# The drive of each scan made on VectorE instead of GpSimd, in a two-layer Mamba, MoE and attention kernel

## The reference

```python
def step(state, xs):
    d_t, B_t, C_t, u_t = xs
    dA = jnp.exp(d_t[..., None] * A)
    state = state * dA + (d_t * u_t)[..., None] * B_t[:, None, :]
    y_t = jnp.einsum('ben,bn->be', state, C_t)
    return (state, y_t)
```

## Time and profile before

| | before |
|---|---|
| median of 3 runs | 905.98 us |
| the profiled execution | 904.61 us |
| its span in the profile | 902.4 us |
| PE busy | 736.9 us (82%) |
| DVE busy | 719.1 us (80%) |
| ACT busy | 436.1 us (48%) |
| POOL busy | 388.9 us (43%) |
| DVE scans, L1002 | 32, 99.1 us, mean 3.10 us |
| DVE read-outs, L1020 | 32, 65.5 us, mean 2.05 us |
| POOL drives, L1365 | 32, 97.8 us, mean 3.06 us |

### The profile page before, as it was taken

How to read it: one execution, slowest core, us unless ns; L and a number is a source line. 1 busy time by engine, 2 the same in 40 slices (tenths; PEclk the granted TensorE clock), 3 DMA queues, 4 the chain that set the end, 5 groups by cost and what they waited for, 6 DMA issues and landing times.

```text
span 902.4 us, 10282 instructions
## 1 busy us (share of the span) xinstructions
PE 736.9 (82%) x3448; PEld 563.3 (62%) x3448; DVE 719.1 (80%) x1151; ACT 436.1 (48%) x836; POOL 388.9 (43%) x291
## 2 busy tenths in 40 slices
PE   5256643577666889999978999998999989899997
PEld 1011112345434667888767888887788877688886
DVE  6999988799999977878758877778777757766665
ACT  5444102544542335444455667675666655433442
POOL 0555545365645233445434545455435524221231
PEclk8667675887978999999999999999979999999999
DMA  6132230334335324444410111111110223433340
GB/s 190 57 101 97 72 105 29 97 122 140 121 112 157 113 89 127 152 146 147 133 49 24 57 32 48 42 46 32 30 43 30 74 56 128 130 106 111 100 131 25
DMA packets 40531, 81.33 MB, mean 90 GB/s; under 512 B 5752, under 2 KB 8064, under 8 KB 40480
## 3 DMA queue, kind: packets, MB, share of 16 engines
q1 hardware_dynamic: 40480, 80.69, 29.0%
HBM read 79.30 MB, written 1.38 MB: 89 GB/s over the span
## 4 chain that ended last, share of the span: by engine, by line
PE 41%; DVE 34%; issue 13%; ACT 9%; POOL 1%; DMA 1%; SPq 0%; DVEq 0%; ACTq 0%; POOLq 0%
PE bank L86 13%; PE bank L87 12%; PE bank L88 12%; DVE state L1002 9%; DVE read_out L1020 5%; ACT probs L867 4%; DVE row_bias L1293 3%; DVE scores L1289 3%; PE bank L577 2%; DVE hidden L1175 1%; ACT q_t_hi L661 1%; ACT w_hi L661 1%; DVE u_sb L927 1%; DVE probs_t_lo L916 1%; DVE x_norm L947 1%
## 5 line engine op out<-in xcount | busy, mean ns | idle before, releaser
L1375 POOL TENSOR_TENSOR w_lo<-w_raw,w_hi 128x768 fp32r<-128x768 f32 (+1 forms) x106 | 195.2, 1843 | 284.2 <-ACT w_hi L661 249.3
L86 PE MATMUL bank<-xt_hi,w_hi 128*128 128x512 f32 x400 | 168.9, 422 | 0.5 <-DVE q_t_lo L916 0.4
L661 ACT ACTIVATE w_hi<-w_raw 128x768 fp32r<-128x768 f32 (+1 forms) x106 | 85.6, 810 | 155.9 <-PE bank L88 121.4
L87 PE MATMUL bank<-xt_lo,w_hi 128*128 128x512 f32 x400 | 160.6, 401 | 0.0
L88 PE MATMUL bank<-xt_hi,w_lo 128*128 128x512 f32 x400 | 160.1, 400 | 0.0
L916 DVE TENSOR_TENSOR hidden_lo<-hidden,hidden_hi 128x512 fp32r<-128x512 f32 x84 | 117.4, 1398 | 51.0 <-ACT hidden_hi L661 50.9
L371 PE MATMUL bank<-read_out,identity 128*128 128x512 f32 x96 | 75.5, 931 | 83.6 <-DVE read_out L1020 55.6
L661 ACT ACTIVATE hidden_hi<-hidden 128x512 fp32r<-128x512 f32 x84 | 52.4, 624 | 145.2 <-DVE hidden L1178 143.2
L1365 POOL TENSOR_TENSOR drive<-delta_u,b_rows 128x1024 f32<-128x1024 f32 x32 | 97.8, 3059 | 36.3 <-DVE state L1002 35.6
L371 PEld LDWEIGHTS bank<-read_out,identity 128*128 128x128 f32 x96 | 23.2, 267 | 128.3 <-DVE read_out L1020 76.4
L1002 DVE TENSOR_TENSOR_SCAN state<-decay_t,drive 128x1024 f32<-128x1024 f32 x32 | 99.1, 3098 | 0.0
(11 more groups left out here) (172 smaller groups left out, 1513.2 us busy)
## 6 DMA issues: line engine op xcount, KB each, us to landing
w_raw<-in_ffn_w SPq DMA_DIRECT2D x74, 384.0 KB, 3.3
b_rows<-bc_scratch SPq DMA_DIRECT2D x32, 256.0 KB, 3.7
c_rows<-bc_scratch SPq DMA_DIRECT2D x32, 256.0 KB, 3.3
route_bc<-route_scratch SPq DMA_DIRECT2D x32, 256.0 KB, 3.6
route_bc<-route_scratch SPq DMA_DIRECT2D x32, 192.0 KB, 3.4
w_raw<-in_attn_proj_w SPq DMA_DIRECT2D x16, 384.0 KB, 3.0
route_bc<-route_scratch SPq DMA_DIRECT2D x32, 128.0 KB, 3.6
w_raw<-in_attn_out_w SPq DMA_DIRECT2D x16, 256.0 KB, 2.6
```

Source lines behind the costliest of these rows:

```text
L86: e.matmul(out, w_hi, m_hi, start=first, stop=False)
L87: e.matmul(out, w_hi, m_lo, start=False, stop=False)
L661: e.activation(out, source, ACT.Copy).then_inc(sem(name), 1)
L1375: e.tensor_tensor(lo[:, 0:n], w_raw[p % RAW][:, 0:n], hi[:, 0:n].bitcast(F32), ALU.subtract).then_inc(sem("w_lo"), 1)
```

## The change

The drive is made by DVE. A new function `scan_drive` in DVE's block has the same waits, operands and semaphore as POOL's `make_drive` had, which is taken out. The first drive of each half stands before its scan; after that the drive of step `n + 1` stands between scan `n` and read-out `n`. POOL keeps its other work. Code of PE, ACT and SP is as it was.

```diff
+            def scan_drive(h, n):
+                if n >= DS:
+                    return
+                i = h * DS + n
+                at.wait_ge("conv", 2 * HALVES)
+                at.wait_ge(f"delta_u{h}", EH)
+                at.wait_ge(f"ld_b{i % 3}", 16 * (i // 3 + 1))
+                at.wait_ge("state", i - 1)
+                e.tensor_tensor(drive[i % 2][:, :, :], delta_u[:, h, :, :],
+                                b_rows[i % 3][:, :].unsqueeze(1).broadcast_to([P, EH, HT]),
+                                ALU.mult).then_inc(sem("drive"), 1)
...
             split_gates()
+            scan_drive(0, 0)
             for n in range(DS):
                 scan_state(0, n)
+                scan_drive(0, n + 1)
                 scan_read(0, n)
...
             move_route(2)
+            scan_drive(1, 0)
             scan_state(1, 0)
+            scan_drive(1, 1)
             scan_read(1, 0)
...
                 if n < DS:
                     scan_state(1, n)
+                    scan_drive(1, n + 1)
...
-            def make_drive(h, n):
...
-            make_drive(0, 0)
-            for n in range(DS):
-                if n + 1 < DS:
-                    make_drive(0, n + 1)
-                if n == 0:
-                    scale_norm(1, 2)
+            scale_norm(1, 2)
...
-            make_drive(1, 0)
-            make_drive(1, 1)
...
-                if n + 1 < DS:
-                    make_drive(1, n + 1)
```

## The result

| | before | changed |
|---|---|---|
| median | 905.75 us (4 runs, 904.04 to 907.22) | 878.29 us (4 runs, 875.5 to 880.02) |
| profiled execution, span | 904.61, 902.4 us | 878.84, 876.8 us |
| DVE busy | 719.1 us, 80% | 692.4 us, 79% |
| POOL busy | 388.9 us, 43% | 295.1 us, 34% |

The ratio is 0.9695, 95% interval 0.9663 to 0.9726: faster by 3.05%. In an independent repetition (the last experiment) it is 0.9701. DVE got 32 products more and is busy 27 us less, because a busy time holds the time in which an instruction stood still.

A forecast was written before the change was run, and what follows sets the result against it. DVE was taken as the bound, held about 2.2 us by each POOL drive. Gains 4.8 + 11.2 + 1.5 + 7.9 = 25.4 us from 904.6 give 879.2, with the median's 1.4 880.6; forecast 880, range 871 to 890.

The forecast's parts named there:

- The price of the drive: One drive on DVE: 1.15 us like a read-out, POOL's 2.23 the far bound; net 1.02 in a step.
- Steps 0 to 2: Start of half 0, up to scan 2: gains 2.85 and 4.0 us, loses 2.0; scan 2 starts 4.8 us sooner.
- the row of the small power: Step 1: POOL's small power overlapped a read-out unhindered by 0.77 us; so 879.2 us, against 880.0 by the lock rule.
- Steps 2 to 15: Rest of half 0: 25.8 us removed, 13.3 and 1.3 added, gain 11.2; a step goes from 5.62 to 4.5 us.
- `softplus_floor(1)`: In half 0's steps: ran inside a drive's time before, now stands alone on DVE and costs 1.3 us.
- The turn of the halves: Between half 0 and half 1: routing gains 3.7 us, 2.2 is paid in SP's queue; gain 1.5.
- Half 1: Second half's units: 24.0 us of POOL's holding goes, 14 drives add 16.1; gain 7.9, `w_lo` as costly as before.
- Half 0 only: Rival: half 0 gains, half 1 doesn't, as PE's sums or ACT's rounding set the pace; 887 us, chance 0.14.
- More cover for `w_lo`: Rival in half 1: `w_lo` may fall under L1175, at most 10 us more gained; 870 us, chance 0.10.
- DVE simply full: Rival: long scans have another cause, so DVE keeps them and gets the drives on top; 938 us, chance 0.04.
- No gain: Rival: a drive on DVE costs near POOL's 2.2 us; about 905 us, chance 0.02.
- The rest: Stretch behind 303 us, after unit 15: no change, 0 us; a changed length would show the prediction wrong.

The follow-up runs named there:

- the last experiment: The changed kernel run once more without a further edit, on the same chip as a later run: 877.66 us, ratio 0.9701 to the kernel before.
- the one-input experiment: Changed kernel plus 32 POOL instructions multiplying one 128x1024 tile by a constant, result unused: 903.83 us, ratio 1.0002 to the kernel before.
- the constant: Changed kernel plus 32 POOL instructions writing a constant into a free 128x1024 tile, reading nothing: 880.17 us, ratio 0.9741 to the kernel before.
- the first experiment: Changed kernel plus 32 two-input POOL products of 128x1024 at the drives' old places, result unused: 938.52 us, ratio 1.0382 to the kernel before.

## Why the prediction was right, step by step

**The price of the drive** was bounded by the read-out's 1.15 and POOL's 2.23 us, and taken at the lower end. It is 1.20 to 1.22 us busy; net it costs 0.98 in a step, forecast 1.02. The reason given for the small net, that the drive covers the read-out's wait, was shown by swapping the two (4.77 us a step). That POOL's reads make DVE stand still, told in the prediction from matching ends, was shown by putting three kinds of work on POOL of which nothing is used; that it is one port is the picture which fits them.

**Steps 0 to 2** gained 5.1, forecast 4.8: scan 0 starts at 30.05 (forecast 30.25), and the eight `z_gate` take 2.67 (forecast 2.7). The forecast sided with the row of the small power, not with a lock for the whole instruction. Here POOL's row of the changed kernel:

```profile
36.61 2.92 POOL L1374 TENSOR_TENSOR rstd<-rstd,half_power 128x4 f32<-128x4 f32 x1 [9.13 <-DVE rstd L941]
```

It ends at 39.53, and the drive of 38.64 takes 1.20 us all the same. The Trainium skill (SBUF — State Buffer, "Who interferes with whom") calls the shared pair an exclusive lock, and says of DVE's 2-port modes that the first to issue keeps it for the whole instruction; the prediction tried this on two-input instructions. There the row above and the one-input experiment (0.84 us of 3.66) disagree with it. Its other sentence, that a two-input DVE instruction contends with a GpSimd instruction that reads and not with one that only writes, is what the product and the constant showed (1.92 us, and nothing). It leaves out the roundings and `z_gate`, which have one input and were held as well. The rounding beside the constant stood until about the constant's end, as a lock for the whole instruction would have it; whether it ran in a 2-port mode no run shows. The 4.0 us of `z_gate` were forecast rightly from rows, not from the two-input picture.

**Steps 2 to 15** gained 10.3, forecast 11.2; this step failed in one term. The step itself is 4.45 (forecast 4.5), but `softplus_floor(1)`, costed at 1.3 us, cost 7.01 - 4.45 = 2.56: from scan 7 at 65.74 to scan 8 at 72.75. Steps are shorter, so DVE reached it before PE and ACT had made its input (0.94 us of idle time), and the pair took 1.61. The prediction named late rows of B and a late ACT at `hidden_lo` as what could go wrong; it did not ask the same of this one-off instruction. One step later the wait is gone. A step 0.05 us cheaper than forecast gave some of this back.

**The turn of the halves** gained 3.1, forecast 1.5. The two parts that were worked out are right: the routing ends 3.73 us earlier (forecast 3.7), and the route loads leave 2.31 us later behind the copy of the routing rows (forecast 2.2). What was left out is the landing: from the issue to L1178/L1190 it was 6.13 us before and is 4.47 after, 4.30 in the repetition. With half 1's drives on POOL it was 4.71, so the order of the drives at this place doesn't make the difference, and in the other traces of kernels in which L1190 still waits for these loads it was 4.3 to 4.5. The 6.13 were seen in the one profiled execution of the kernel before; whether it is scatter or has a cause stays open. Without these 1.7 us the turn gains 1.4, against the forecast 1.5. The queue behind it was shown by moving the loads: 5.4 us.

**Half 1** gained 8.2, forecast 7.9. The lines of the changed kernel from 149.48 to 274 us (count, busy us, mean ns, idle before):

```profile
L1014 DVE TENSOR_TENSOR_SCAN state<-decay_t,drive 128x1024 f32<-128x1024 f32 x15 | 34.3, 2284 | 0.0
L1005 DVE TENSOR_TENSOR drive<-delta_u,b_rows 128x1024 f32<-128x1024 f32 x14 | 29.4, 2102 | 0.0
L916 DVE TENSOR_TENSOR hidden_lo<-hidden,hidden_hi 128x512 fp32r<-128x512 f32 x15 | 21.6, 1438 | 0.0
L1032 DVE TENSOR_TENSOR read_out<-state,c_rows 128x1024 f32<-128x1024 f32 x14 | 17.0, 1211 | 0.0
```

The excess is 14 x (2.10 - 1.20) = 12.6 on the drives and 15 x (1.44 - 0.68) = 11.4 on `hidden_lo`, together 24.0 us, 1.60 for each of 15 `w_lo`. That is the price the forecast left in place, and it split the 48.0 us of the earlier trace rows rightly. The read-outs, which were to keep part of it, are all at 1.21: the drive stands in the place where `w_lo` asks. Which instruction is held changes, the price of a `w_lo` doesn't.

**The rivals.** Half 0 only: refuted, the stretch of half 1 shrank by 8.2 us, with DVE busy 126.00 of 126.51. More cover for `w_lo`: refuted by the 24.0 us. DVE simply full: refuted by the first experiment. That this experiment also measured the rival's 938 us is a coincidence of two other sums. No gain: refuted by the drive's 1.2 us.

**The rest**, costed at nothing, took 1.1 us more; in the repetition it took 1.2 less than before (598.5 against 599.74). The prediction named a changed length of this stretch as a sign of being wrong; with both signs seen for one kernel, it is scatter of single executions.

## What to carry to other kernels

Before work is given to GpSimd for being free, look at the instructions of VectorE beside it that read SBUF, those with two inputs first: if they are longer than the same shape elsewhere, the excess is the price, and it counts wherever VectorE sets the end, however idle GpSimd looks. The test is a product of which nothing uses the result; the comparison to make is VectorE's own time (here 1.0 to 1.2 us) against the time held (1.9 to 2.2), not against GpSimd's. When a stretch gets shorter, ask again of each one-off instruction in it whether its input is made by then, and of the DMA queue whether what the next stage needs first stands behind waits of the stage before.

## What the runs showed of the hardware

- What a POOL instruction holds goes with what it reads. A two-input product of 128x1024 into f32 held DVE for 2.15 to 2.23 us, one of other inputs into fp32r 1.92; a `w_lo` of 128x768 1.60; one large input 0.84, though that instruction took 3.66 us; 128x4 nothing in 2.92 us; a constant written to 128x1024 nothing, as far as DVE's two-input instructions go.
- Of DVE's one-input instructions, a rounding of 128x32 took 2.33 us beside a product and 0.76 beside a constant, alone 0.17; eight `z_gate` of 128x256 took 6.72 beside two products and 3.01 beside the last 0.6 us of a constant, alone 2.67. With an input in PSUM none was held: L1175 took 0.67 us beside a drive on POOL.
- The scan is held like a product (4.44 us against 2.28), and so is a routing step of 128x128 (L1078 2.42 us, the same step now 0.29): a short instruction pays as much as a long one.
- On DVE a dependent instruction starts 0.13 to 0.18 us later than an independent one in its place (2.33 against 2.20 us behind a scan, 1.31 against 1.13 behind a drive). An instruction placed between two dependent ones costs that much less.
